# Cross-attention with broadcast add on one core: row order of two weight loads, number of warm-up transposes, one more reload by rows

## The chip, the cores and the metric

One core of a Trainium2 chip. The metric is the device time of one execution in microseconds (us); the kernel before has three timed executions and one further one that the hardware profiler recorded.

## The reference, cut to what matters

```python
# x, ctx: [32, 512, 512] f32; Wq, Wk, Wv: [512, 512] f32; 16 heads of 32
q = (x @ Wq.T), k = (ctx @ Wk.T), v = (ctx @ Wv.T)     # split into heads
probs = softmax(q k^T / sqrt(32));  att = probs v       # per batch
return x + att[0]                                       # batch 0's attention, added to all 32 batches
```

Only batch 0 of the attention is used, so the arithmetic is that of one batch. The traffic is not: x is read once (33.5 MB) and the result written once (33.5 MB), beside 4 MB for one batch of ctx and the three weights.

## The kernel before, in words

The 512 rows of a batch are four blocks ("rows" j = 0..3 of the program). Partition p holds rows 2p and 2p+1 of each half (j = 0, 1 are half 0, j = 2, 3 are half 1). x is held in 18 slots of 1 MB: slot g holds two batches of one half. Half 0 fills slots 0 to 15, half 1 goes into slots 16, 17 and then 0 to 15 again, group g of half 1 into slot (16 + g) mod 18, each as soon as the half 0 result there has been stored.

Start. POOL writes the identity `ident`, PE runs WARM_UP transposes of it (L529), then turns weights, ctx and batch 0 of x on PE (`turn`, L364) into PSUM. ACT copies each turned block out (`empty`, L639 to L641), and for operands that are split in a high and a low part DVE writes the low part (L723). Keys (`key_chunk`, L393), queries (`query_chunk`, L373) and values (`value_chunk`, L404) follow, each of four chunks, queries of one pass and the two others of three. PE's order is written out by hand.

Attention. For each j: scores (L417), row maximum on DVE (L728), exponential on ACT (L647), transposes of the probabilities on PE (L439), their copy on ACT (L656), the product with v (L450), the turn back (L462), and `normalize` on DVE (L754, L758). The attention of j = 0 comes in two halves of columns (units FIRST and SECOND), that of j = 1, 2, 3 whole (ROW_1, ROW_2, ROW_3).

Adds and transfers. POOL (L319, L328, L336) and DVE (L767, L774, L784) add a unit to the slots. All DMAs are issued by SP in one order written by hand: the seven first loads (L251 to L258), the loads of x (`load`, L209; `load_batch`, L213), stores of FIRST in FIRST_ORDER, then stores of SECOND in SECOND_ORDER with, from the sixth on, one `reload_row(0, ...)` (L238) behind each. Then for g = 0..15 a store of ROW_1, and from g = 5 a `reload(g - 3)` behind each. `reload_row(0, g)` loads row 0 of half 1's group g as soon as the SECOND store of the old slot has landed; groups outside BY_ROWS are loaded whole by `reload` (L209). Last come the stores of half 1 (L232 by rows, L224 whole). SP waits for `added` before a store and for `stored` before a reload, and everything behind a waiting DMA waits with it.

The names that the change touches: WARM_UP, BY_ROWS, SECOND_ORDER, `dest` (where ACT and DVE put a turned block) and the DMAs of wq and wv. A weight tile is [128 partitions, 4, 512], and `turn("wq_t", i)` turns the rows `wq_raw[:, i, :]`, so `dest` has to put them in the columns that those rows have in `wq_t`.

Of the kernel before, what the change touches and what calls it, by code (L numbers as in the profile page):

```python
# [11 lines left out]
P = 128  # L12
# [7 lines left out]
def cross_attention_add(nc, x, ctx, wq, wk, wv, out):  # L20
# [7 lines left out]
    T = N // P  # L28
# [6 lines left out]
    S_BANKS = 4  # L35
    PT_BANK, BACK_BANK, ATT_T_BANK = 4, 6, 7
    PT_SLOTS = 6
    WARM_UP, KEEP_UP = 24, 16
    SCALE = float(DK) ** -0.5
    HI, LO = 0, 1  # L40
    PASSES = ((HI, HI), (HI, LO), (LO, HI))
# [9 lines left out]


    FRESH = SLOTS - GROUPS
    BY_ROWS = range(FRESH, FRESH + 12)
    ADDED_BY_ROWS, STORED_BY_ROWS = (1, 2, 3, 4, 5, 6, 7, 8), (1, 2, 3, 4)
    LAST_ROW_DVE_GROUPS = (5, 6, 7, 8, 1, 2, 3, 4)
    WHOLE_POOL_GROUPS = (9, 11, 13, 15)
# [1 line left out]
    LAST_STORE_ORDER = (5, 6, 7, 8, 1, 2, 3, 4, 0, 9, 10, 11, 12, 13, 14, 15)  # L59

    FIRST_ORDER = (1, 3, 0, 5, 2, 4, 7, 6, 8, 9, 10, 11)
    SECOND_ORDER = (1, 3, 0, 5, 2, 7, 9, 4, 11, 6, 8, 10, 13, 12, 15, 14)
    assert T == 4 and C == 4 and HG == 4 and N == 512 and D == HEADS * DK

    x_rows = x.rearrange("b (j p r) d -> p j b r d", p=P, r=ROWS)
# [2 lines left out]
    with ExitStack() as stack:  # L68
        def sb(name, shape, dtype=F32, where=stack):
            return where.enter_context(nc.sbuf_tensor(name, shape, dtype))  # L70

        def sem(name):
            return stack.enter_context(nc.semaphore(name))
# [5 lines left out]
        with ExitStack() as early:  # L79
            sb("low_slots", [P, WQ_RAW, BPS, ROWS, D], where=early)  # L80
            wq_raw = sb("wq_raw", [P, C, D], where=early)
            wk_raw = sb("wk_raw", [P, C, D], where=early)
            ctx_raw = sb("ctx_raw", [P, T, D], where=early)
            wv_raw = sb("wv_raw", [P, C, D], where=early)
            wk_t = sb("wk_t", [P, C, 2, D], F32R, where=early)
            ctx_t = sb("ctx_t", [P, C, 2, N], F32R, where=early)
            wv_t = sb("wv_t", [P, C, 2, D], F32R, where=early)
# [10 lines left out]
        wq_t = sb("wq_t", [P, C, D])  # L98
        k_t = sb("k_t", [P, HG, 2, N], F32R)
# [11 lines left out]
        x0_loaded, wq_loaded, ctx_loaded, wv_loaded = (  # L111
            sem(n) for n in ("x0_loaded", "wq_loaded", "ctx_loaded", "wv_loaded"))
        wk_first_loaded, wk_rest_loaded = sem("wk_first_loaded"), sem("wk_rest_loaded")
        loaded = [[sem(f"loaded{J}_{g}") for g in range(GROUPS)] for J in range(T // ROWS)]
        row_2_loaded = {g: sem(f"row_2_loaded{g}") for g in BY_ROWS}
        row_2_added = {g: sem(f"row_2_added{g}") for g in ADDED_BY_ROWS}
# [17 lines left out]
        for j in range(2, T):  # L134
            JOBS += [("x0_t", j, ATT_T_BANK), ("q", j, ATT_T_BANK), ("q_t", j, ATT_T_BANK)]
        number = {(what, i): n for n, (what, i, _) in enumerate(JOBS)}

        SPLIT = ("wk_t", "ctx_t", "wv_t", "k_t", "q_t")
# [6 lines left out]
        def dest(what, i, half=HI):  # L145

            if what == "x0_t":
                return x0_t
            if what == "q":
                return q_raw  # L150
            if what == "q_t":
                return q_t[:, i % 2, :, half, :]
            if what == "wq_t":
                return wq_t[:, :, i * P:(i + 1) * P]
            if what == "wk_t":
                return wk_t[:, :, half, i * P:(i + 1) * P]
            return {"ctx_t": ctx_t, "wv_t": wv_t, "k_t": k_t}[what][:, i, half, :]

        def as_dest(ps, to):
            return ps.rearrange("p (c n) -> p c n", n=P) if len(to.shape) == 3 else ps  # L160
# [46 lines left out]
        def _(sp):  # L207
# [7 lines left out]
            def store(unit, g):  # L215
                sp.wait_ge(added[g], steps(unit, g))
                r, cols = unit // ROW_1, cols_of(unit, g)
                sp.dma_start(out_rows[:, 0, 2 * g:2 * g + 2, r, cols], rows_of(0, g, r, cols)).then_inc(stored[g], 16)
# [16 lines left out]
            def reload_row(r, g):  # L235
                old = slot_of(LAST_HALF, g)
                sp.wait_ge(stored[old], steps(SECOND if r == 0 else ROW_1, old) * 16)
                sp.dma_start(rows_of(LAST_HALF, g, r), x_rows[:, LAST_HALF, 2 * g:2 * g + 2, r, :]).then_inc(  # L238
                    row_2_loaded[g] if r == 0 else loaded[LAST_HALF][g], 16)

            def reload(g):
                if g in BY_ROWS:
                    reload_row(1, g)
                else:
                    old = slot_of(LAST_HALF, g)
                    sp.wait_ge(stored[old], steps(ROW_1, old) * 16)
                    load(LAST_HALF, g)

            wq_rows = wq.rearrange("(t p) d -> p t d", p=P)
            wk_rows = wk.rearrange("(t p) d -> p t d", p=P)  # L250
            sp.dma_start(wk_raw[:, 0, :], wk_rows[:, 0, :]).then_inc(wk_first_loaded, 16)  # L251
            sp.dma_start(ctx_raw[:, :, :], ctx[0].rearrange("(p t) d -> p t d", p=P)).then_inc(ctx_loaded, 16)
            sp.dma_start(wk_raw[:, 1:, :], wk_rows[:, 1:, :]).then_inc(wk_rest_loaded, 16)
            sp.dma_start(wq_raw[:, :, :], wq_rows).then_inc(wq_loaded, 16)
            sp.dma_start(slots[:, 0, 0, :, :], x_rows[:, 0, 0, :, :]).then_inc(x0_loaded, 16)
            sp.dma_start(wv_raw[:, :, :], wv.rearrange("(t p) d -> p t d", p=P)).then_inc(wv_loaded, 16)

            sp.dma_start(slots[:, 0, 1, :, :], x_rows[:, 0, 1, :, :]).then_inc(loaded[0][0], 16)  # L258
            for g in range(1, GROUPS):
# [22 lines left out]
            for g in FIRST_ORDER:  # L282
                store(FIRST, g)
            for n, g in enumerate(SECOND_ORDER):
                store(SECOND, g)
                if n >= ROW_LAG:
                    reload_row(0, FRESH + SECOND_ORDER[n - ROW_LAG])
            for g in SECOND_ORDER[GROUPS - ROW_LAG:len(BY_ROWS)]:
                reload_row(0, FRESH + g)
# [17 lines left out]
        def _(pool):  # L307
# [14 lines left out]
            for g in ADDED_BY_ROWS:  # L322
                if g in BY_ROWS:
                    pool.wait_ge(row_2_loaded[g], 16)
# [6 lines left out]
            for g in WHOLE_POOL_GROUPS:  # L331
                if g in BY_ROWS:
                    pool.wait_ge(row_2_loaded[g], 16)
# [299 lines left out]
        def _(act):  # L633
            def empty(what, i):

                act.wait_ge(bank_filled, number[what, i] + 1)
                ps, to = job_bank(what, i), dest(what, i)
                if what == "q":
                    nc.scalar.mul(to, ps, SCALE).then_inc(act_evacuated, 1)  # L639
                else:  # L640
                    nc.scalar.copy(to, as_dest(ps, to)).then_inc(act_evacuated, 1)  # L641
# [71 lines left out]
        def _(dve):  # L713
            def empty(what, i):

                ps = job_bank(what, i)
                if what == "v":
                    dve.wait_ge(bank_filled, number[what, i] + 1)
                    nc.vector.tensor_copy(v[:, i, :], ps).then_inc(dve_evacuated, 1)
                else:  # L720
                    high, low = dest(what, i, HI), dest(what, i, LO)
                    dve.wait_ge(act_evacuated, sum(BY_ACT[:number[what, i] + 1]))
                    nc.vector.tensor_tensor(low, as_dest(ps, low), high.bitcast(F32),  # L723
                                            ALU.subtract).then_inc(dve_evacuated, 1)
# [52 lines left out]
            def add_whole(g):  # L777
                dve.wait_ge(att_ps_ready, ROW_3)
                if g in BY_ROWS:
                    dve.wait_ge(row_2_loaded[g], 16)  # L780
# [106 lines left out]
```

## Time and profile before

| | before |
|---|---|
| timed executions | 186.40, 186.23, 185.81 us, median 186.23 |
| profiled execution, its own time | 185.45 us |
| its span | 183.6 us, mean granted TensorE clock 0.893 |
| busy PE / DVE / ACT / POOL | 72% / 56% / 53% / 42% of the span |
| HBM read, written | 37.75 MB, 33.55 MB, 388 GB/s over the span |
| DMA packets | 31168, 71.52 MB |

The span is what the profiler saw of the program; the own time is 1.85 us longer. A busy share is an average over stages with different limits, so the table alone does not say what bounds a stage. Rates of a stretch come with the share of time in which the 16 DMA engines were busy; that share can read a little over 1.

### The profile page before, as it was taken

What the parts mean: (1) busy time and instruction counts of PE and PEld (TensorE: products, weight loads), DVE (VectorE), ACT (ScalarE), POOL (GpSimd) and SP (SyncE); (2) the same over time, 40 slices, a digit from 0 to 9 for tenths busy, and PEclk for the clock granted to TensorE, in tenths of its full rate; (3) what the DMA queues carried; (4) which work ended last, traced back from release to release, by engine and by line L of the source; (5) the groups of instructions that cost most, each with busy time, mean ns of one, the idle gap of its engine ahead of it and who ended that gap; (6) DMA issues with size and microseconds to landing.
All of it is one profiled execution on the core that took longest, in us unless ns stands there. A gap on an engine that the chain in (4) does not pass through costs nothing.

```text
span 183.6 us, 3367 instructions
## 1 busy us (share of the span) xinstructions
PE 132.1 (72%) x1240; PEld 92.4 (50%) x1240; DVE 102.4 (56%) x163; ACT 97.2 (53%) x225; POOL 77.8 (42%) x41
## 2 busy tenths in 40 slices
PE   6999999999989998998987998899887000000000
PEld 6878858677656675556765556566565000000000
DVE  0444135634759399934499677685541999920000
ACT  2525526468668469867898668797974000000000
POOL 1000000000039299600039999259995899910000
PEclk9999999999999999999999999999999755555555
DMA  6999999999999998999999999999999999999998
GB/s 211 361 378 417 408 411 411 409 411 406 409 409 401 384 370 298 370 397 400 408 403 405 393 355 397 403 408 408 403 416 405 387 406 407 384 401 404 409 407 320
DMA packets 31168, 71.52 MB, mean 390 GB/s; under 512 B 1840, under 2 KB 7984, under 8 KB 31024
## 3 DMA queue, kind: packets, MB, share of 16 engines
q1 hardware_dynamic: 31152, 71.31, 101.1%
q8 instruction: 10, 0.16, 0.3%
q14 instruction: 6, 0.05, 0.1%
HBM read 37.75 MB, written 33.55 MB: 388 GB/s over the span
## 4 chain that ended last, share of the span: by engine, by line
PE 55%; DVE 13%; ACT 12%; issue 6%; DVEq 1%; POOL 0%; ACTq 0%; POOLq 0%
PE bank L439 13%; PE bank L417 8%; PE bank L373 7%; PE bank L450 7%; PE bank L393 6%; ACT probs L647 6%; PE bank L404 6%; DVE slots L784 5%; ACT probs_t L656 4%; PE bank L364 4%; DVE neg_max L728 3%; DVE slots L774 3%; PE bank L529 2%; PE bank L626 1%; DVEq L68 1%
## 5 line engine op out<-in xcount | busy, mean ns | idle before, releaser
L319 POOL TENSOR_TENSOR slots<-slots,att_rows 128x512 f32<-128x512 f32 (+1 forms) x23 | 40.5, 1794 | 73.9 <-DVE att_rows L754 73.9
L728 DVE TENSOR_REDUCE neg_max<-bank 128x1 f32<-128x512 f32 x64 | 41.6, 682 | 19.1 <-PE bank L417 18.8
L647 ACT ACTIVATE probs<-bank,neg_max 128x512 f32<-128x512 f32 x64 | 44.6, 698 | 10.8 <-DVE neg_max L728 10.3
L439 PE MATMUL bank<-ident,probs 128*128 128x128 f32 x256 | 40.7, 283 | 6.2 <-ACT probs L647 5.8
L656 ACT COPY probs_t<-bank 128x512 f32<-128x512 f32 x62 | 36.4, 590 | 12.5 <-PE bank L439 8.3
L439 PEld LDWEIGHTS bank<-ident,probs 128*128 128x128 f32 x256 | 27.8, 140 | 24.5 <-ACT probs L647 17.7
L417 PE MATMUL bank<-k_t,q_t 32*128 32x512 f32 x192 | 24.4, 426 | 0.1
L328 POOL TENSOR_TENSOR slots<-slots,att_rows 128x1024 f32<-128x1024 f32 x8 | 18.6, 2370 | 5.6 <-DVE att_rows L754 5.6
L336 POOL TENSOR_TENSOR slots<-slots,att_rows 128x2048 f32<-128x2048 f32 x4 | 18.0, 4532 | 3.0 <-DVE att_rows L754 3.0
L767 DVE TENSOR_TENSOR slots<-slots,bank 128x512 f32<-128x512 f32 (+1 forms) x21 | 18.5, 906 | 0.0
L450 PE MATMUL bank<-probs_t,v 128*32 128x128 f32 x496 | 17.3, 276 | 1.5 <-ACT probs_t L656 1.4
L417 PEld LDWEIGHTS bank<-k_t,q_t 32*128 32x128 f32 x192 | 12.2, 183 | 8.4 <-issue 4.7
L373 PE MATMUL bank<-wq_t,att_rows 128*128 128x512 f32 x32 | 16.0, 596 | 0.0
L450 PEld LDWEIGHTS bank<-probs_t,v 128*32 128x32 f32 x496 | 13.0, 109 | 5.3 <-ACT probs_t L656 2.9
L393 PE MATMUL bank<-ctx_t,wk_t 128*128 128x512 f32 x48 | 13.3, 409 | 0.3 <-DVE ctx_t L723 0.2
L404 PE MATMUL bank<-wv_t,ctx_t 128*128 128x512 f32 x48 | 13.3, 409 | 0.0
L647 ACT ACTIVATION_READ_ACCUMULATOR probs<-bank,neg_max 128x1 f32 x64 | 13.3, 208 | 0.0
L740 DVE COPY att_t<-bank 128x128 f32<-128x128 f32 x16 | 4.6, 287 | 10.8 <-PE bank L450 10.8
L393 PEld LDWEIGHTS bank<-ctx_t,wk_t 128*128 128x128 f32 x48 | 8.3, 189 | 2.2 <-issue 0.5
L404 PEld LDWEIGHTS bank<-wv_t,ctx_t 128*128 128x128 f32 x48 | 8.3, 189 | 2.0 <-issue 0.7
L774 DVE TENSOR_TENSOR slots<-slots,bank 128x1024 f32<-128x1024 f32 x8 | 9.1, 1216 | 0.0
L784 DVE TENSOR_TENSOR slots<-slots,bank 128x2048 f32<-128x2048 f32 x4 | 8.9, 2281 | 0.0
(46 smaller groups left out, 95.6 us busy)
## 6 DMA issues: line engine op xcount, KB each, us to landing
slots<-in_x_dram SPq DMA_DIRECT2D x18, 1024.0 KB, 17.3
slots<-in_x_dram SPq DMA_DIRECT2D x28, 512.0 KB, 9.4
out_dram<-slots SPq DMA_DIRECT2D x28, 512.0 KB, 9.4
out_dram<-slots SPq DMA_DIRECT2D x12, 1024.0 KB, 12.3
out_dram<-slots SPq DMA_DIRECT2D x24, 256.0 KB, 6.4
ctx_raw<-in_ctx_dram SPq DMA_DIRECT2D x1, 1024.0 KB, 4.9
wq_raw<-in_L_xattn_Wq_dram SPq DMA_DIRECT2D x1, 1024.0 KB, 9.2
wv_raw<-in_L_xattn_Wv_dram SPq DMA_DIRECT2D x1, 1024.0 KB, 12.1
```

What stands on the lines that cost most here:

```text
L319: nc.gpsimd.tensor_tensor(xs, xs, a.unsqueeze(1).to_broadcast([P, BPS, a.shape[1]]), ALU.add).then_inc(added[g], 1)
L328: nc.gpsimd.tensor_tensor(xs, xs, att.unsqueeze(1).to_broadcast([P, BPS, D]), ALU.add).then_inc(row_2_added[g], 1)
L373: last = mm(job_bank("q", j), x0_t[:, c, :], wq_t[:, c, :], start=(c == 0), stop=(c == C - 1))
L393: last = mm(job_bank("k_t", g), wk_t[:, c, a, g * P:(g + 1) * P], ctx_t[:, c, b, :], start=(c == 0 and (a, b) == PASSES[0]), stop=(c == C ...
L404: last = mm(job_bank("v", t), ctx_t[:, c, a, t * P:(t + 1) * P], wv_t[:, c, b, :], start=(c == 0 and (a, b) == PASSES[0]), stop=(c == C - ...
L417: last = mm(bank[:, h % S_BANKS, :], q_t[rows, j % 2, g, a, :], k_t[rows, g, b, :], start=((a, b) == PASSES[0]), stop=((a, b) == PASSES[-1]))
L439: last = nc.tensor.transpose(bank[:, PT_BANK + h % 2, t * P:(t + 1) * P], probs[:, h % 2, t * P:(t + 1) * P], ident[:, :])
L450: last = mm(att_t_ps[i * DK:(i + 1) * DK, g, :], v[:, t, h * DK:(h + 1) * DK], place_of_probs_t(j, h)[:, t, :], start=(t == 0), stop=(t == ...
L647: nc.scalar.activation(probs[:, h % 2, :], bank[:, h % S_BANKS, :], ACT.Exp, bias=neg_max[:, h:h + 1], scale=1.0, accum_out=row_sum[:, h:h ...
L656: nc.scalar.copy(place_of_probs_t(j, h), bank[:, PT_BANK + h % 2, :].rearrange("p (t n) -> p t n", t=T)).then_inc(probs_t_ready, 1)
L728: nc.vector.tensor_reduce(neg_max[:, h:h + 1], bank[:, h % S_BANKS, :], AX_X, ALU.max, negate=True).then_inc(max_ready, 1)
L767: nc.vector.tensor_tensor(xs, xs, a.unsqueeze(1).to_broadcast([P, BPS, a.shape[1]]), ALU.add).then_inc(added[g], 1)
```

## The change

wq and wv are loaded with four adjacent rows to a partition (row 4p + t at [p, t]) in place of rows 128 apart (row 128t + p at [p, t]), as ctx is already. The copies out of PSUM put the columns apart: ACT writes wq_t with a step of four elements, ACT and DVE write the two parts of wv_t so. wk stays as it was. The warm-up has 17 transposes, not 24. BY_ROWS takes in group 14, whose rows go into slot 12, and SECOND_ORDER stores slot 12 before slot 13.

```diff
-    WARM_UP, KEEP_UP = 24, 16
+    WARM_UP, KEEP_UP = 17, 16
-    BY_ROWS = range(FRESH, FRESH + 12)
+    BY_ROWS = range(FRESH, FRESH + 13)
-    SECOND_ORDER = (1, 3, 0, 5, 2, 7, 9, 4, 11, 6, 8, 10, 13, 12, 15, 14)
+    SECOND_ORDER = (1, 3, 0, 5, 2, 7, 9, 4, 11, 6, 8, 10, 12, 13, 15, 14)
             if what == "wq_t":
-                return wq_t[:, :, i * P:(i + 1) * P]
+                return wq_t[:, :, i::T]
             if what == "wk_t":
                 return wk_t[:, :, half, i * P:(i + 1) * P]
-            return {"ctx_t": ctx_t, "wv_t": wv_t, "k_t": k_t}[what][:, i, half, :]
+            if what == "wv_t":
+                return wv_t[:, i, half, :].rearrange("p (n t) -> p t n", t=T)
+            return {"ctx_t": ctx_t, "k_t": k_t}[what][:, i, half, :]
-            wq_rows = wq.rearrange("(t p) d -> p t d", p=P)
-            sp.dma_start(wq_raw[:, :, :], wq_rows).then_inc(wq_loaded, 16)
+            sp.dma_start(wq_raw[:, :, :], wq.rearrange("(p t) d -> p t d", p=P)).then_inc(wq_loaded, 16)
-            sp.dma_start(wv_raw[:, :, :], wv.rearrange("(t p) d -> p t d", p=P)).then_inc(wv_loaded, 16)
+            sp.dma_start(wv_raw[:, :, :], wv.rearrange("(p t) d -> p t d", p=P)).then_inc(wv_loaded, 16)
```

On SP, behind the last SECOND stores and ahead of the ROW_1 stores, the kernel before has two row reloads in a row:

```order
32 L218 DMA out_dram<-slots 128x2x512
33 L238 DMA slots<-in_x_dram 128x2x512 x2
34 L218 DMA out_dram<-slots 128x2x512 x6
...
54 L218 DMA out_dram<-slots 128x2x512
55 L238 DMA slots<-in_x_dram 128x2x512 x2
56 L209 DMA slots<-in_x_dram 128x2x1024 x2
57 L232 DMA out_dram<-slots 128x2x512 x4
```

and the changed kernel, whose lines are numbered two higher, has

```order
32 L220 DMA out_dram<-slots 128x2x512
33 L240 DMA slots<-in_x_dram 128x2x512 x3
34 L220 DMA out_dram<-slots 128x2x512 x6
...
54 L220 DMA out_dram<-slots 128x2x512
55 L240 DMA slots<-in_x_dram 128x2x512 x3
56 L211 DMA slots<-in_x_dram 128x2x1024
57 L234 DMA out_dram<-slots 128x2x512 x4
```

Half a megabyte of reading has moved from the whole reload at row 56 to the gap ahead of the ROW_1 stores at row 33; the other half stays at its place as a row reload.

## Rows read from the trace of the kernel before

**Rows 1.** The page: DMA share in tenths and rate in 40 slices of 4.59 us
```profile
DMA  6999999999999998999999999999999999999998
GB/s 211 361 378 417 408 411 411 409 411 406 409 409 401 384 370 298 370 397 400 408 403 405 393 355 397 403 408 408 403 416 405 387 406 407 384 401 404 409 407 320
```

**Rows 2.** Windows: stretch, its length, busy us by engine, PE clock, DMA share, GB/s
```profile
2.00:14.00 12.00, 11.68 (x71) 10.12 (x71) 4.46 (x7) 3.80 (x9) 0.00 (x0) 1.00 0.98 368
14.00:58.00 44.00, 42.64 (x338) 31.09 (x336) 22.79 (x41) 27.19 (x61) 4.64 (x4) 1.00 1.03 410
72.00:74.00 2.00, 1.82 (x40) 1.34 (x38) 2.00 (x5) 2.00 (x6) 2.00 (x2) 1.00 0.62 202
145.00:183.60 38.60, 0.00 (x0) 0.00 (x0) 16.59 (x11) 0.00 (x0) 16.08 (x4) 0.50 0.99 390
146.00:182.00 36.00, 0.00 (x0) 0.00 (x0) 15.60 (x11) 0.00 (x0) 15.08 (x4) 0.50 1.02 404
```

**Rows 3.** Timeline of SP's DMA issues: start us, length us, line, operands, count
```profile
0.74 0.39 SPq L251 DMA_DIRECT2D wk_raw<-in_L_xattn_Wk_dram  x1
1.19 0.42 SPq L252 DMA_DIRECT2D ctx_raw<-in_ctx_dram  x1
...
3.21 0.45 SPq L256 DMA_DIRECT2D wv_raw<-in_L_xattn_Wv_dram  x1
...
54.65 15.80 SPq L218 DMA_DIRECT2D out_dram<-slots  x18
...
87.61 1.79 SPq L238 DMA_DIRECT2D slots<-in_x_dram  x2
96.69 6.05 SPq L218 DMA_DIRECT2D out_dram<-slots  x6
...
144.98 4.13 SPq L224 DMA_DIRECT2D out_dram<-slots  x4
```

**Rows 4.** SP's waits in 128:150: waiting line, releaser, us, times, longest
```profile
SPq L223 <- DVE slots L774: 9.7, 4, 7.8
```

**Rows 5.** Timeline of PE, ACT and DVE from the start to the first key chunk
```profile
1.52 4.28 PE L529 MATMUL bank<-ident 128*128 128x128 f32 x24 [1.52 <-POOL ident L310]
5.63 0.60 PE L364 MATMUL bank<-ident,wk_raw 128*128 128x128 f32 x4
6.13 1.97 PE L364 MATMUL bank<-ident,ctx_raw 128*128 128x128 f32 x16
6.27 0.59 ACT L641 CAST wk_t<-bank 128x512 fp32r<-128x512 f32 x1 [4.25 <-PE bank L364]
6.88 0.69 DVE L723 TENSOR_TENSOR wk_t<-bank,wk_t 128x512 fp32r<-128x512 f32 x1 [6.88 <-ACT wk_t L641]
7.49 2.47 DVE L723 TENSOR_TENSOR ctx_t<-bank,ctx_t 128x512 fp32r<-128x512 f32 x4
```

**Rows 6.** One line's instructions, 1.7:4.2 of L529 and 5.6:8 of L364
```profile
L529 PE MATMUL bank<-ident x13: 421/421/476, 1.5 to 4.1; 128*128 128x128 f32 x13
L364 PE MATMUL bank<-ident,ctx_raw x16: 272/273/328, 6.1 to 7.8; 128*128 128x128 f32 x16
```

**Rows 7.** DMA issues of the page: KB each, us from issue to landing
```profile
ctx_raw<-in_ctx_dram SPq DMA_DIRECT2D x1, 1024.0 KB, 4.9
...
wv_raw<-in_L_xattn_Wv_dram SPq DMA_DIRECT2D x1, 1024.0 KB, 12.1
```

**Rows 8.** Timelines around the last value weights: PE, ACT and DVE
```profile
28.10 0.65 PE L364 MATMUL bank<-ident,att_rows 128*128 128x128 f32 x4 [0.25 <-ACT att_rows L639]
...
29.82 3.00 PE L404 MATMUL bank<-wv_t,ctx_t 128*128 128x512 f32 x12
27.94 0.58 ACT L641 CAST wv_t<-bank 128x512 fp32r<-128x512 f32 x1
30.23 0.62 ACT L641 CAST wv_t<-bank 128x512 fp32r<-128x512 f32 x1
30.88 0.69 DVE L723 TENSOR_TENSOR wv_t<-bank,wv_t 128x512 fp32r<-128x512 f32 x1 [0.18 <-ACT wv_t L641]
```

## The prediction

> **What bounds the kernel now.** I read the slices of the page first. The DMA engines read 9 tenths busy in all slices but the first, the 16th and the last, at about 400 GB/s [rows 1], so it looks like a kernel bound by its 71.5 MB. The windows then show where the queue still runs out. The 14th and 15th slices move 384 and 370 GB/s [rows 1], and 72 to 74 us only 202 at a share of 0.62 [rows 2]. The timeline of SP says why: 18 stores of 256 KB are issued in 15.80 us [rows 3], 4.72 MB / 15.80 us = 299 GB/s, less than the engines take away. They catch up with the issues, whatever they had queued before. The start of those stores, 54.65 us, is set by the first attention, not by transfers.
>
> The same happens at the end. SP waits 7.8 us for DVE's first adds of the last row [rows 4] and issues the first of the last stores at 144.98 [rows 3]. Those are twelve stores of 1 MB and four of 0.5 MB, 14.68 MB. From 145 us on 38.6 x 0.390 = 15.05 MB are moved [rows 2], so only 0.37 MB, about 0.9 us of work, was still queued when SP came with new stores. From there the end is fixed: 14.68 MB at 404 GB/s [rows 2] are 36.3 us. So **the time is that of the compute chain up to the first add of the last row, near 145 us, plus a fixed drain**, and transfers have only just kept up. To win, the compute chain has to come earlier; transfers alone have almost nothing to win.
>
> The chain begins at 1.52 us with the warm-up. The 24 transposes end in the four of wk at 5.63, and those of ctx start at 6.13 [rows 5]; ctx was issued at 1.19 [rows 3] and took 4.9 [rows 7], so it landed at 6.1, when PE was just done. From there PE, ACT and DVE run with few gaps.
>
> **The change, part by part.**
>
> *Warm-up, 24 to 17.* 13 of the warm-up transposes start from 1.5 to 4.1 us, 2.6 / 12 = 0.22 us apart; the 16 of ctx start from 6.1 to 7.8, 1.7 / 15 = 0.11 apart [rows 6]. That is the clock's two levels, 1.2 and 2.4 GHz, and in this execution it rose shortly after 4.1 us. With 17, the last three or so run fast: wk's four start near 4.9 in place of 5.63 and are over near 5.3. Then PE waits for ctx until 6.13. What this gives: ACT's copy of wk (6.27 to 6.86) and DVE's low part of it (6.88 to 7.57) leave the way of the ctx blocks. ctx's first block could be on ACT 0.64 us after its transposes start, as wk's was (5.63 to 6.27), at 6.77, and on DVE 0.61 later at 7.38, where it was at 7.49 [rows 5]. **Gain 0.1 us** in the execution that is profiled.
>
> The three timed executions were 0.36, 0.78 and 0.95 us slower than the profiled one. The trace does not show why. One cause is a later rise of the clock. The bound: with all 24 + 4 transposes 0.22 apart, ctx would start at 1.52 + 28 x 0.22 = 7.7 us, 1.55 us late; with 17 + 4 at 1.52 + 21 x 0.22 = 6.1, not late at all. The gain of this part thus lies between 0.1 and 1.6 us. I take 0.6, nearer to the lower end, because the slowest of the timed executions is only 0.95 above the one whose price I know, and because a part of what is lost at the slow clock after 6.1 us stays lost.
>
> *wq and wv by adjacent rows.* The DMAs of ctx, already in this form, and of wq and wv are of the same 1 MB. 2 to 14 us, where the weights load, runs at 368 GB/s, against 410 behind it [rows 2]: 12 x (410 - 368) / 410 = 1.2 us of transfer time lost in all. wq and wv are 2.1 of its 4.4 MB, so their form can give back at most 0.6 us; at the other end the new form costs as much as ctx may have cost in the same window, 0.3 us. I take 0.2 us earlier. No engine waits for it: wv, the later of the two, landed 12.1 us after 3.21, near 15.3 [rows 3, 7], and PE turns the last of it between 28 and 30 us [rows 8]. Behind it, the queue is refilled by SP and runs dry again near 72 us, as above. On the path: **0**.
>
> *The copies that put columns apart.* ACT makes four copies of wq and four of wv, DVE four low parts of wv. The rows show 0.58 to 0.62 us on ACT and 0.69 on DVE [rows 8] for unit steps; none shows a step of four elements, 16 bytes, on the writing side. Bounds: nothing, or twice the time if each element is paid alone. PE's matmuls read the same tiles in unit steps and do not change. I take nothing, since 512 elements per partition in 0.6 us are about one a nanosecond, which already looks like one element at a time. If the cover is gone, see the second rival.
>
> *The 13th row reload, and slot 12 ahead of 13.* The extra 0.5 MB is issued behind the two at 87.61, in the gap of SP between 89.4 and 96.69 us [rows 3]. It waits for the store of slot 12, which now has the place that slot 13 had. The queue is then 0.52 MB / 400 GB/s = 1.3 us longer when the ROW_1 stores come at 96.69. Behind those six, which end near 102.7, the first reload of row 1 needs the store of slot 0 landed; with 1.3 us more in the queue that is still about in time, and a wait of some tenths would be covered by the queue. Later SP issues 0.5 MB less at the whole reloads. Bytes stay, the stretch from 74 to 144 us is never empty in the slices [rows 1], and a fuller queue there gives at most part of the 0.9 us of queue left at 145. In that time the new stores' first packets would hardly have come anyway: the very first DMA was issued at 0.74 [rows 3], and the first slice's 211 GB/s are 0.97 MB, 2.4 of its 4.59 us at 410, as if nothing had moved before 2.2 us [rows 1]. **0**, between -0.2 and +0.2.
>
> **Sum.** In the profiled execution 185.45 - 0.1 = 185.35 us. The median of the timed ones is 186.23, and there I expect 186.23 - 0.6 = **185.6 us**, a ratio of 0.997. About 0.3%, 0.56 us, is what a measurement of this kernel can tell from no change, so the forecast sits at that edge.
>
> **Rivals.**
>
> *The warm-up gives its 0.1 us and no more.* If the timed executions are slower for another reason than the clock (a slower HBM, the ends of the program), only the 0.1 us remains: 186.1. For it: no row ties the clock to the 0.78 us. Against: the cold spacing of 0.22 us over 28 transposes makes just a spread of this size.
>
> *The columns put apart cost double on ACT and DVE.* ACT's wv copies would be 1.2 us, DVE's 1.4. Two of wv's ACT copies, and those of q_t and x between them, now stand within 27.94 to 30.85 [rows 8]; with three doubled ones the last would end near 32.5, DVE's near 33.9 in place of 31.57. PE's fourth value chunk starts at about 29.82 + 9 x 0.25 = 32.1 and would wait 1.8 us, and everything to the end with it: 185.6 + 1.8 = 187.4, **slower**. It decides from a copy of about 0.8 us, since DVE now ends 0.5 us ahead of that chunk. The trace excludes neither end. The Trainium skill, "Advanced Engine Details and Errata", section "SBUF Cachelines", says lines are 16 bytes, that at least two hits on one are needed, and that a different one per access costs. By it, this rival holds, since a step of four f32 touches a new line with each element; a table of its own price is not given, and no row here shows it.
>
> *The clock rises later, because PE stands idle.* PE would now wait 0.8 us, from about 5.3 to 6.13, which it did not before. If the rise to 2.4 GHz then comes only behind the ctx transposes, these cost 16 x 0.11 = 1.8 us more: 187.4, slower. Against: the clock rose soon after 4.1 us [rows 6], and up to there PE is as busy as before; and idle stretches of PE such as the 0.25 us ahead of 28.10 [rows 8] did not lower it.
>
> *Transfers decide after all.* If the queue at 145 us is worth its whole 0.9 us, then 0.2 us of wq and wv and the fuller queue near 104 us, where a slice shows 355 GB/s [rows 1], count too: 4.59 x (405 - 355) / 405 = 0.6 us more, 185.0.
>
> **How the numbers follow.** Forecast 0.42; the warm-up alone, near 186.1, 0.27; transfers too, near 185.0, 0.13; double copies 0.07; late clock 0.07; some other small loss, up to 186.8, 0.04. Faster by over 0.3% (under 185.67) takes somewhat over half of the forecast's case, nearly all of the transfers' and a little of the warm-up alone: 0.43. Slower by over 0.3% is the two slow rivals and the rest, 0.16. The remaining 0.41 is within 0.3%. The range goes from 184.8 (186.23 - 1.4, nearly the whole bound of the warm-up) to 186.8; above it lie the two rivals at 187.4, 0.14 together.
>
> **What would show it.** Right: 17 transposes, wk's four near 4.9 us or ahead of 6.0 in any case, ctx's at 6.1 and 0.11 us apart, the DVE low part of ctx at 7.4; wv's copies unchanged at 0.6 and 0.7 us; the first last-row store at 144.9 or a little before, and 404 GB/s behind it; the share still low at 72 to 74. Wrong: copies of over 0.8 us and a gap on PE ahead of L406 near 32 us; ctx transposes 0.22 apart; or a first last-row store no earlier than 145.0 with a shorter drain behind it, which would mean that transfers bound the end.

## The result and the profile after

| | before | changed |
|---|---|---|
| median of the timed executions | 186.07 us (185.33 to 186.64) | 186.84 us (186.52 to 188.98) |
| ratio | 1 | 1.0051, 95% interval 1.0031 to 1.007 |
| profiled execution, own time | 185.45 us | 187.16 us |
| its span | 183.6 us | 185.4 us |

The change makes the kernel 0.5% slower, about 0.95 us by the ratio; the two medians differ by 0.77 us. The forecast was 0.3% faster, so it is wrong in sign, and the measured median is 0.04 us above the forecast's range.

The windows of the changed kernel, columns as in [rows 2]:

```profile
2.00:14.00 12.00, 11.86 (x59) 10.04 (x59) 4.56 (x7) 3.92 (x8) 0.00 (x0) 1.00 1.00 396
14.00:58.00 44.00, 42.23 (x335) 30.64 (x334) 22.50 (x37) 29.51 (x57) 2.88 (x3) 1.00 1.00 389
72.00:74.00 2.00, 2.00 (x14) 1.30 (x14) 2.00 (x5) 2.00 (x6) 2.00 (x3) 1.00 1.04 331
```

The weights do load faster, 396 GB/s in place of 368. What is gained is then lost again: 389 in place of 410 behind it. About half of that is missing between 44 and 50 us, first before, then changed (most of the rest is missing between 50 and 58 us):

```profile
44.00:50.00 6.00, 5.68 (x65) 4.16 (x67) 2.87 (x5) 3.99 (x10) 0.00 (x0) 1.00 1.03 409
44.00:50.00 6.00, 6.00 (x42) 4.47 (x40) 2.37 (x4) 3.76 (x10) 0.00 (x0) 1.00 0.88 326
```

SP may issue the next loads of x only when PE has used up the buffers that they go into; here it issues them at 46.85, not at 45.08. It is the late PE that lets the queue run low: with the same faster loads and PE on time (experiment 7) this window moves 406 GB/s, with the old loads and PE 1.7 us late (experiment 10) it moves 369. SP's issues stand to [rows 3] like this:

```profile
56.42 15.35 SPq L220 DMA_DIRECT2D out_dram<-slots  x18
...
146.72 4.12 SPq L226 DMA_DIRECT2D out_dram<-slots  x4
```

The first stores of all come 1.77 us later than at 54.65, and the first store of the last row 1.74 us later than at 144.98. Everything that this execution lost, it lost before 56 us; the whole of it arrives at the last row and at the end (187.16 - 185.45 = 1.71 us). PE's timeline shows two places, to be held against [rows 5] and [rows 8]:

```profile
1.52 3.89 PE L531 MATMUL bank<-ident 128*128 128x128 f32 x17 [1.52 <-POOL ident L312]
5.20 1.06 PE L366 MATMUL bank<-ident,wk_raw 128*128 128x128 f32 x4
6.27 2.59 PE L366 MATMUL bank<-ident,ctx_raw 128*128 128x128 f32 x16
8.88 1.64 PE L395 MATMUL bank<-ctx_t,wk_t 128*128 128x512 f32 x6
...
30.82 2.55 PE L406 MATMUL bank<-wv_t,ctx_t 128*128 128x512 f32 x9 [0.21 <-issue]
33.63 0.93 PE L406 MATMUL bank<-wv_t,ctx_t 128*128 128x512 f32 x3 [0.27 <-DVE wv_t L725]
34.50 0.97 PE L419 MATMUL bank<-k_t,q_t 32*128 32x512 f32 x12
```

The first place is the clock: ctx's 16 transposes take 2.59 us where they took 1.97, because in this execution the clock rose only while they ran. The first key chunk starts 0.56 us late (8.88 in place of 8.32), of which 0.14 had passed when ctx's first transpose started. It is a matter of when the clock rises in the one execution that is profiled, and not of the form of the weights: PE also ran slow past 5 us in experiment 3, which has the old form. The second is new: PE starts the value chunks 1.00 us late, about half of it new, and has to stop ahead of the fourth for DVE's low part of wv. The scores that stood at 32.75 start at 34.50. Of these 1.75 us 0.56 were there at the first key chunk and 1.2 belong to this stretch. ACT and DVE show why:

```profile
28.49 1.09 ACT L643 CAST wv_t<-bank 128x512 fp32r<-128x512 f32 x1
29.34 0.66 ACT L643 CAST q_t<-bank 128x512 fp32r<-128x512 f32 x1
29.88 1.11 ACT L643 CAST wv_t<-bank 128x512 fp32r<-128x512 f32 x1
30.75 0.67 ACT L643 COPY att_rows<-bank 128x512 f32<-128x512 f32 x1
31.29 1.10 ACT L643 CAST wv_t<-bank 128x512 fp32r<-128x512 f32 x1
```

```profile
27.38 1.09 DVE L725 TENSOR_TENSOR wv_t<-bank,wv_t 128x512 fp32r<-128x512 f32 x1 [1.95 <-ACT wv_t L643]
31.21 2.28 DVE L725 TENSOR_TENSOR wv_t<-bank,wv_t 128x512 fp32r<-128x512 f32 x2
```

A copy that writes with a step of four takes 1.09 to 1.11 us where it took 0.6, a low part 1.1 where it took 0.69 [rows 8]. The copies of q_t and x between them, which write in unit steps, stay near 0.6. So the second rival has happened, at 1.85 times the duration on ACT and 1.6 times on DVE, not twice. The experiments had to show that this, and not the clock or the queue, is the loss of the median too.

### The profile page after: what moved, and what is told of

Read it like the earlier page. It is cut to its first block, busy times and chain, and to the rows that moved or that the text cites. A ratio compares the mean times of both kernels' runs of the same rounds, so it can differ in the third digit from the quotient of the medians.

```text
span 185.4 us, 3354 instructions
## 1 busy us (share of the span) xinstructions
PE 133.6 (72%) x1233; PEld 92.8 (50%) x1233; DVE 103.9 (56%) x163; ACT 100.9 (54%) x225; POOL 77.8 (42%) x41
## 4 chain that ended last, share of the span: by engine, by line
PE 54%; ACT 13%; DVE 13%; issue 6%; DVEq 1%; POOL 0%; ACTq 0%; POOLq 0%
PE bank L441 13%; PE bank L419 7%; PE bank L375 7%; PE bank L452 7%; PE bank L395 6%; ACT probs L649 6%; PE bank L406 5%; PE bank L366 5%; DVE slots L786 5%; ACT probs_t L658 4%; DVE neg_max L730 3%; DVE slots L776 3%; PE bank L531 2%; ACT wv_t L643 2%; PE bank L628 1%
## 5 line engine op out<-in xcount | busy, mean ns | idle before, releaser
L441 PE MATMUL bank<-ident,probs 128*128 128x128 f32 x256 | 40.7, 283 | 6.2 <-ACT probs L649 5.8
L406 PE MATMUL bank<-wv_t,ctx_t 128*128 128x512 f32 x48 | 13.8, 413 | 0.5 <-DVE wv_t L725 0.3
```

Of the source, the lines that this page charges most:

```text
L406: last = mm(job_bank("v", t), ctx_t[:, c, a, t * P:(t + 1) * P], wv_t[:, c, b, :], start=(c == 0 and (a, b) == PASSES[0]), stop=(c == C - ...
L441: last = nc.tensor.transpose(bank[:, PT_BANK + h % 2, t * P:(t + 1) * P], probs[:, h % 2, t * P:(t + 1) * P], ident[:, :])
```

## The experiments

Each kernel of experiments 1 to 11 is the kernel before with the edit shown, timed against the kernel before on the same chip.

**1. Only the new form of both weights.** The change's loads and `dest` for wq and wv, with warm-up 24 and 12 reloads.

```diff
-                return wq_t[:, :, i * P:(i + 1) * P]
+                return wq_t[:, :, i::T]
+            if what == "wv_t":
+                return wv_t[:, i, half, :].rearrange("p (n t) -> p t n", t=T)
-            wq_rows = wq.rearrange("(t p) d -> p t d", p=P)
+            wq_rows = wq.rearrange("(p t) d -> p t d", p=P)
-            sp.dma_start(wv_raw[:, :, :], wv.rearrange("(t p) d -> p t d", p=P)).then_inc(wv_loaded, 16)
+            sp.dma_start(wv_raw[:, :, :], wv.rearrange("(p t) d -> p t d", p=P)).then_inc(wv_loaded, 16)
```

> The kernel before with only wq and wv loaded by adjacent rows and the columns put apart at the copies. Theory A (the copies with a step of four elements are what costs): ACT's copies of wq and wv take 1.09 us and DVE's low parts of wv 1.1 as in the changed kernel, the first store of the last row comes about 1.2 us later than 144.98, and the ratio is about 1.006. Theory B (the shorter warm-up leaves the clock low for longer, and that costs): ratio within 0.002 of 1. Theory C (the 13th reload or the order of slots 12 and 13 costs): ratio within 0.002 of 1.

Measured: 187.96 us against 186.13, ratio 1.0091 (1.0058 to 1.0123). The form alone costs more than the whole change. Its profiled execution, 188.52 us, must not be read as its price. ctx took 6.9 us to land, not 4.9, and PE waited for it; with the same loads ctx took 4.9 to 5.0 us in the changed kernel and in experiments 7, 8 and 12, so this is put down to the one execution:

```profile
ctx_raw<-in_ctx_dram SPq DMA_DIRECT2D x1, 1024.0 KB, 6.9
```

```profile
8.08 1.97 PE L366 MATMUL bank<-ident,ctx_raw 128*128 128x128 f32 x16 [0.90 <-DMA ctx_raw<-in_ctx_dram]
```

**2. All but the new form.**

```diff
-    WARM_UP, KEEP_UP = 24, 16
+    WARM_UP, KEEP_UP = 17, 16
-    BY_ROWS = range(FRESH, FRESH + 12)
+    BY_ROWS = range(FRESH, FRESH + 13)
-    SECOND_ORDER = (1, 3, 0, 5, 2, 7, 9, 4, 11, 6, 8, 10, 13, 12, 15, 14)
+    SECOND_ORDER = (1, 3, 0, 5, 2, 7, 9, 4, 11, 6, 8, 10, 12, 13, 15, 14)
```

> The changed kernel with the loads and copies of wq and wv as before: 17 warm-up transposes, 13 row reloads, slot 12 ahead of 13. Theory A: 0.2 to 0.6 us faster than before, ratio 0.997 to 0.999. Theory B or C: ratio 1.003 to 1.006, as the whole change.

Measured: 185.67 us against 186.13, ratio 0.9968 (0.9944 to 0.9991). Theory A holds, and B and C fall: the rest of the change is a gain of about 0.6 us. 1.0091 x 0.9968 = 1.0059, which is the measured 1.0051 within its interval. The change is the sum of a loss and a smaller gain.

**3. Only the warm-up.**

```diff
-    WARM_UP, KEEP_UP = 24, 16
+    WARM_UP, KEEP_UP = 17, 16
```

> Only the warm-up cut from 24 to 17. Theory A: ratio 0.997 to 0.999, ctx transposes start near 6.1 us whenever the clock rises. Theory B: ctx transposes 0.22 us apart for some of their length, first key chunk later than 8.32 us, ratio above 1.002.

Measured: 185.76 us against 186.13, ratio 0.9978 (0.9952 to 1.0005). Within what was expected, though its interval just reaches 1. PE's start reads

```profile
1.52 3.89 PE L529 MATMUL bank<-ident 128*128 128x128 f32 x17 [1.52 <-POOL ident L310]
5.20 1.00 PE L364 MATMUL bank<-ident,wk_raw 128*128 128x128 f32 x4
6.15 1.97 PE L364 MATMUL bank<-ident,ctx_raw 128*128 128x128 f32 x16
```

All 17 and most of wk's run slow here, and ctx's still start at 6.15, when ctx has landed: the wait for ctx takes up the slow part.

**4. A step of two in place of four.** Two adjacent rows to a partition, in two halves.

```diff
-                return wq_t[:, :, i * P:(i + 1) * P]
+                return wq_t[:, :, i // 2 * 2 * P + i % 2:(i // 2 + 1) * 2 * P:2]
+            if what == "wv_t":
+                return wv_t[:, i, half, :].rearrange("p (h n r) -> p h r n", h=2, r=2)
-            wq_rows = wq.rearrange("(t p) d -> p t d", p=P)
+            wq_rows = wq.rearrange("(h p r) d -> p h r d", p=P, r=2)
```

(Not shown: wv's load, the side of `wq_raw` and `wv_raw` in both loads, and the copies' view of the bank likewise)

> wq and wv with two adjacent rows to a partition and two such halves, so that the copies write with a step of two elements, 8 bytes; warm-up and reloads as before. If what costs is that each element touches a new 16-byte line (the Trainium skill, Advanced Engine Details and Errata, SBUF Cachelines, asks for two hits on a line), the copies take 0.59 and 0.69 us as for unit steps and the ratio is within 0.002 of 1. If any step other than one is paid, they take 1.09 us and the ratio is about 1.006.

Measured: ratio 1.0008 (0.998 to 1.0035). The groups by shape, with count, busy us and mean ns of one:

```profile
L645 ACT COPY wq_t<-bank 128x512 f32<-128x512 f32 x4 | 2.5, 626 | 1.6 <-PE bank L368 1.6
L645 ACT CAST wv_t<-bank 128x512 fp32r<-128x512 f32 x4 | 2.5, 636 | 1.6 <-PE bank L368 1.6
L727 DVE TENSOR_TENSOR wv_t<-bank,wv_t 128x512 fp32r<-128x512 f32 x4 | 2.8, 689 | 3.3 <-ACT wv_t L645 3.3
```

At 8 bytes from one element to the next ACT pays 0.04 us and DVE nothing; at 16 bytes both pay 0.4 to 0.5. ACT's copies only write with the step. DVE's low part also reads the high part of wv_t with it, so for DVE no run tells writing from reading. That is how the Trainium skill tells it ("Advanced Engine Details and Errata", SBUF Cachelines: 16-byte lines, two hits on one for full speed). Steps of two and four bear it out; no other step was tried. "SBUF — State Buffer" (the note on cachelines in its section on the DMA port swizzle) counts a stride of four f32 as still free, though it too asks for two hits on a line. Here the measurement says that a step of four is not free.

**5. Only wv.**

```diff
+            if what == "wv_t":
+                return wv_t[:, i, half, :].rearrange("p (n t) -> p t n", t=T)
-            sp.dma_start(wv_raw[:, :, :], wv.rearrange("(t p) d -> p t d", p=P)).then_inc(wv_loaded, 16)
+            sp.dma_start(wv_raw[:, :, :], wv.rearrange("(p t) d -> p t d", p=P)).then_inc(wv_loaded, 16)
```

> Only wv is loaded by adjacent rows and copied with a step of four; wq, the warm-up and the reloads as before. The last value weights stand right ahead of the value chunks, so the theory that the copies of wv are what delays PE expects nearly all of the loss of both together: ratio 1.006 to 1.009, value chunks starting or pausing 1 us or more later than 29.82. The rival, that the wq copies with their place among the key copies cost as much, expects 1.003 to 1.005.

Measured: 187.75 us against 186.35, ratio 1.0094 (1.0059 to 1.013): all of the loss. PE's timeline:

```profile
24.09 1.88 PE L375 MATMUL bank<-wq_t,att_rows 128*128 128x512 f32 x4
...
31.00 2.55 PE L406 MATMUL bank<-wv_t,ctx_t 128*128 128x512 f32 x9 [0.22 <-issue]
33.84 0.93 PE L406 MATMUL bank<-wv_t,ctx_t 128*128 128x512 f32 x3 [0.29 <-DVE wv_t L725]
34.71 0.97 PE L419 MATMUL bank<-k_t,q_t 32*128 32x512 f32 x12
```

The query chunks start 0.71 us late (23.38 before; the clock again), the scores 1.96 us late (32.75 before). Between the two lies the price of the wv copies on the path, 1.25 us. The first store of the last row stands at 146.95, 1.97 us late: nothing is won back or lost behind it. 1.25 us are 0.67%, within the interval. But they lie near its lower end, and near that of experiment 1: by the ratios the two lost 1.75 and 1.7 us, and none of their 14 executions is less than 1.87 us above the fastest of the kernel before. Whether the form costs more than 1.25 us in them, or the clock rose late in all of them, stays open.

**6. Only wq.**

```diff
-                return wq_t[:, :, i * P:(i + 1) * P]
+                return wq_t[:, :, i::T]
-            wq_rows = wq.rearrange("(t p) d -> p t d", p=P)
+            wq_rows = wq.rearrange("(p t) d -> p t d", p=P)
```

> Only wq is loaded by adjacent rows and copied with a step of four. ACT has idle stretches of about 0.5 us between these copies, so the theory expects the longer copies to be hidden: ratio within 0.002 of 1, query chunks starting near 23.38. The rival expects 1.003 to 1.005, with PE waiting ahead of a key or query chunk.

Measured: ratio 1.0000 (0.9975 to 1.0026), and the copies cost the same as wv's:

```profile
18.12 2.21 ACT L641 COPY wq_t<-bank 128x512 f32<-128x512 f32 x2 [0.55 <-PE bank L364]
20.12 0.63 ACT L641 CAST k_t<-bank 128x512 fp32r<-128x512 f32 x1
21.06 1.09 ACT L641 COPY wq_t<-bank 128x512 f32<-128x512 f32 x1 [0.31 <-PE bank L364]
```

The same 0.5 us four times over, and PE's query chunks start at 23.39. ACT had idle time between these copies, and key chunks stand on PE behind each. A copy of nearly twice the time costs only where PE's next work needs it.

**7. Put apart on the reading side.** wq turned by chunks of d, as wv is; ACT and DVE read the bank with a step and write in unit steps.

```diff
-                return wq_t[:, :, i * P:(i + 1) * P]
+                return wq_t[:, i, :].rearrange("p (n t) -> p n t", t=T)
+            if what in ("wq_t", "wv_t"):
+                return ps.rearrange("p (t n) -> p n t", t=T)
-                    elif what in ("wq_t", "wk_t"):
+                    elif what == "wk_t":
```

(Not shown: `dest` of wv, the loads of experiment 1, and the calls that take the new view of the bank)

> wq and wv by adjacent rows, but the columns are put apart where the copies read: ACT and DVE read the bank with a step of 128 elements and write the tile in unit steps (wq turned by chunks of d, as wv is). If only the step on the SBUF writing side is paid, the copies take 0.59 and 0.69 us and the ratio is within 0.002 of 1. If steps in PSUM are paid as well, they take 1 us or more and the ratio is 1.006 or more.

Measured: ratio 1.0001 (0.9977 to 1.0025). ACT and DVE are back at their durations:

```profile
L645 ACT CAST wv_t<-bank 128x512 fp32r<-128x512 f32 x4 | 2.4, 594 | 1.6 <-PE bank L368 1.6
L727 DVE TENSOR_TENSOR wv_t<-bank,wv_t 128x512 fp32r<-128x512 f32 x4 | 2.8, 689 | 3.2 <-ACT wv_t L645 3.2
```

A step of 128 elements in PSUM is free on reading. And with the copies as fast as before, the faster load of both weights (397 GB/s in 2 to 14 us) gives nothing that can be told: the ratio is 1 within 0.25%.

**8. Put apart by PE.**

```diff
-                    last = nc.tensor.transpose(ps[:, m * P:(m + 1) * P], raw, ident[:, :])
+                    out_cols = ps[:, m::T] if what in ("wq_t", "wv_t") else ps[:, m * P:(m + 1) * P]
+                    last = nc.tensor.transpose(out_cols, raw, ident[:, :])
```

(Not shown: wq turned by chunks of d, and the loads of experiment 1)

> wq and wv by adjacent rows, with the columns put apart by PE: each transpose writes its 128 columns of the bank with a step of four elements (wq turned by chunks of d), and ACT and DVE copy in unit steps; warm-up and reloads as before. If a step on PE's side is free, the 32 transposes stay 0.11 us apart and the ratio is within 0.002 of 1. If it is paid, as the Trainium skill says of steps in PSUM (Advanced Engine Details and Errata, PSUM Cachelines), they take about twice as long, 32 x 0.11 = 3.5 us of PE, and the ratio is 1.01 or more.

Measured: ratio 1.0004 (0.9981 to 1.0028), and the 16 transposes of wv take 272 ns each, as those of ctx in [rows 6]:

```profile
L365 PE MATMUL bank<-ident,wv_raw 128*128 128x128 f32 x16 | 2.4, 272 | 0.0
```

A step of 16 bytes is free for PE's f32 transposes into PSUM, so the rule that the expectation quoted does not hold for them. The page gives no factor; "about twice" was an estimate.

**9. Only the 13th reload, with slot 12 ahead of 13.**

```diff
-    BY_ROWS = range(FRESH, FRESH + 12)
+    BY_ROWS = range(FRESH, FRESH + 13)
-    SECOND_ORDER = (1, 3, 0, 5, 2, 7, 9, 4, 11, 6, 8, 10, 13, 12, 15, 14)
+    SECOND_ORDER = (1, 3, 0, 5, 2, 7, 9, 4, 11, 6, 8, 10, 12, 13, 15, 14)
```

> Only the 13th row reload and slot 12 ahead of slot 13. The theory that transfers ahead of the last row do not decide expects a ratio within 0.002 of 1. The rival, that the fuller queue counts, expects 0.997 or less; a cost of the longer queue for the stores behind it would show as 1.003.

Measured: ratio 0.9986 (0.9963 to 1.0009). Inside what the theory expects; a gain of up to 0.4% or a loss of 0.1% is not excluded.

**10. 40 warm-up transposes.**

```diff
-    WARM_UP, KEEP_UP = 24, 16
+    WARM_UP, KEEP_UP = 40, 16
```

> 40 warm-up transposes in place of 24, nothing else. The theory that PE's chain from its first real transpose on sets the end: the 16 more take 1.76 us or more at 0.11 us each, ctx starts near 7.9 us where the clock has risen by then, the first store of the last row comes 1.7 us later than 144.98, and the ratio is 1.006 to 1.011. The rival, that transfers set the end and PE has slack: under 1.004.

Measured: 187.37 us against 186.14, ratio 1.0072 (1.0044 to 1.0099).

```profile
7.82 1.91 PE L364 MATMUL bank<-ident,ctx_raw 128*128 128x128 f32 x16
```

```profile
146.74 4.09 SPq L224 DMA_DIRECT2D out_dram<-slots  x4
```

ctx starts 1.69 us late, the last row's first store comes 1.76 us late, and the profiled execution is 187.10, 1.65 us above the one of before. A delay at the start passes through all 140 us of the chain undiminished: there is no slack in it.

**11. 8 warm-up transposes.**

```diff
-    WARM_UP, KEEP_UP = 24, 16
+    WARM_UP, KEEP_UP = 8, 16
```

> 8 warm-up transposes, nothing else: PE stands idle for over 1.5 us ahead of ctx. If idle time ahead of ctx keeps the clock low for longer, ctx's transposes are 0.22 us apart for most of their length and more follows: ratio above 1.002 and first key chunk over 1 us later than 8.32. If only the number ahead of ctx counts, it is as with 17: ratio 0.996 to 1.000.

Measured: 186.93 us against 186.14, ratio 1.0038 (1.0014 to 1.0062), slower. The profiled execution is its fastest, 185.83 us, and looks as with 17:

```profile
1.52 1.97 PE L529 MATMUL bank<-ident 128*128 128x128 f32 x8 [1.52 <-POOL ident L310]
3.52 1.11 PE L364 MATMUL bank<-ident,wk_raw 128*128 128x128 f32 x4
6.15 1.97 PE L364 MATMUL bank<-ident,ctx_raw 128*128 128x128 f32 x16 [1.52 <-DMA ctx_raw<-in_ctx_dram]
```

The clock had risen when ctx began. The timed ones reach 187.96. Something costs them up to 2 us, and a clock that is still low in ctx's transposes and the key chunks is the candidate; the trace shows one execution only, so this is argued, not shown. Fewer is not better: 8 loses, 17 gains, 24 lies between, 40 loses.

**12. The change, mended.** The edits of experiments 7 and 2 together (not shown again): copies that read with a step, 17 warm-up transposes, 13 reloads.

> The whole change with one thing mended: wq and wv by adjacent rows, 17 warm-up transposes, 13 row reloads, but the copies read the bank with a step and write the tile in unit steps. If the step on the writing side was all that made the change slow, it is as fast as the change without the new form of the weights: ratio 0.995 to 0.999, first store of the last row near 144.9 us. If earlier loads of the weights are worth anything on top, it is below 0.9968; if not, the same.

Measured: 185.56 us against 186.14, ratio 0.9964 (0.994 to 0.9988). It is faster than both kernels, by 0.36% and, over the two ratios, 1.0051 / 0.9964, by 0.9% than the changed one. It is as fast as experiment 2, which keeps the old form of the weights (0.9968). No gain of the new form shows even when its copies cost nothing.

## Why the prediction was wrong, point by point

- **What bounds the kernel.** Right for the compute chain, and shown by the traces of experiments 5 and 10: 1.96 us of delay at the scores, 1.25 of them from the copies, and 1.7 us of delay at ctx arrive whole at the last row and at the end. The drain is less fixed than it was said to be, see below.
- **The warm-up, 0.6 us.** Not contradicted: 0.4 us alone (0.9978), 0.6 with the reload (0.9968). The interval of the first goes from a gain of 0.9 to a loss of 0.1, so it does not tell 0.6 from the 0.1 of the first rival; that of the second, 0.2 to 1.0, does, but has the reload in it. The 0.6 was chosen between two bounds, so that it fits is in part luck. The bound of 1.55 us was argued from a late rise of the clock. Such executions exist: experiment 8's, with 24 transposes, has ctx 1.21 us behind the 6.13 of [rows 5] and took 186.86 us.

```profile
7.34 1.91 PE L365 MATMUL bank<-ident,ctx_raw 128*128 128x128 f32 x16
```

  Experiment 3's timeline has a late rise with 17 and starts ctx on time. The changed kernel's has one later still, ctx at 6.27 and its transposes partly slow; that part is lost with 17 as well.
- **Weights by adjacent rows, 0 on the path.** Right for the transfers: they came sooner, and experiments 4, 7 and 8 show ratios of 1.0001 to 1.0008, none with an interval beyond 0.35% from 1.
- **The copies, "I take nothing".** This is the step that failed. The reason given, that one element a nanosecond "already looks like one element at a time", said nothing about what a line of memory costs. The nearest rows were unit-step copies, and they could not exclude the upper bound of twice. The measured value is 1.09 to 1.11 us where unit steps took 0.59 and 0.69, and PE waits for it ahead of and within the value chunks. The text had the right mechanism as its second rival, with the rule that speaks for it, and gave it 0.07. Its price of 1.8 us was too high on the path of the profiled executions, 1.25 us; the timed ones of experiments 1 and 5 do not exclude it. The copies were taken as 1.2 and 1.4 us end to end, but took 1.1, and ACT began the next instruction 0.85 us after the start of such a copy (28.49 to 29.34 in the changed kernel), so DVE was through sooner than the 33.9 that the rival gave.
- **13th reload, 0.** Within -0.4% and +0.1%. Not told apart from nothing.
- **The sum.** -0.6 for warm-up and reload, +1.25 for the copies of wv on the chain, gives +0.65 us. The whole change measured +0.95, with an interval of 0.6 to 1.3.
- **The late clock as a rival.** That the idle time of PE ahead of ctx by itself delays the rise was not borne out with 17 (0.9978), but a kernel with still more idle time, experiment 11, is slower. How much idle time is harmless was not settled.

One reading was too strong. "Transfers alone have almost nothing to win" holds for the profiled execution of before. In others the 18 stores near 55 us take longer to issue and move less, as in experiment 9's; the last line is the window of before:

```profile
54.62 17.15 SPq L218 DMA_DIRECT2D out_dram<-slots  x18
```

```profile
58.00:72.00 14.00, 13.40 (x115) 8.97 (x116) 10.29 (x20) 9.69 (x23) 10.61 (x10) 1.00 0.99 343
58.00:72.00 14.00, 13.36 (x115) 8.96 (x116) 10.30 (x20) 9.69 (x23) 10.61 (x10) 1.00 1.07 375
```

17.15 us against 15.80 in [rows 3]. There the first store of the last row stands at 144.98, as before, and the execution still took 186.16 us, 0.7 more than the one of before. Experiments 3 and 11 show the same, with 17.19 and 17.21 us for these stores and 0.3 and 0.4 us more in all. From the first store of the last row to the end of the execution the kernel before, the changed one and eight of the experiments take 40.3 to 40.6 us, experiment 4's 40.7, and these three 40.8 to 41.2. So up to 0.7 us of the difference between two executions can come from transfers and not from the clock. Why these stores are slower in one execution than in another stays open.

## What to carry to other kernels

When an edit changes the layout of a load, look at the copy that has to undo it: its step on the SBUF side decides (writing for ACT; for DVE writing and reading were not told apart), and the same rearrangement on the PSUM side, read by ACT and DVE or written by PE, was free here. Price such a copy by where its reader stands: the longer copies of wq were hidden behind key chunks, those of wv stood right ahead of the value chunks and cost 1.25 us in the trace. And where two bounds of an unknown duration differ by a factor of two and a stated rule names the upper one, do not take the lower one on a plausible sentence.

## What the runs showed of the hardware

- 512 f32 elements per partition from PSUM into SBUF, ACT's copy and DVE's subtraction that makes the low part: unit steps in SBUF 0.59 and 0.69 us; 8 bytes apart 0.63 and 0.69; 16 bytes apart 1.09 and 1.09. DVE also reads one operand from SBUF with the same step.
- Steps in PSUM cost nothing in these runs: reads 512 bytes apart on ACT and DVE (0.59 and 0.69 us), and PE's f32 transposes written 16 bytes apart (272 ns, 0.11 us from one to the next).
- The moment at which TensorE's clock rises differs from execution to execution of one start: just after 4.1 us in the profiled execution of before, and within ctx's transposes, behind 6.27 us, in that of the changed kernel.
